# Graph network kernel, layer three: three sign rows on two row groups of TensorE in place of one block of 67 rows

## The reference

```
h = maximum(layernorm(x), 0)
x = x + L2(h, adj)

# inside L2, for every pair of nodes i, j (c = 1):
sub   = mobius_add(-h_i, h_j)
arg   = clip(norm(sub), 0, 1 - 1e-5)
log   = 2 / lam_i * arctanh(arg) * sub / norm(sub)
agg_i = sum_j (adj_ij / deg_i) * log_ij
```

## Time and profile before

| what | value |
|---|---|
| median of three runs | 1149.5 us |
| the profiled execution's own time | 1147.67 us |
| its span, first to last instruction | 1145.9 us |
| TensorE busy, share of the span | 1076.3 us, 94% |
| VectorE busy | 874.6 us, 76% |
| ScalarE busy | 765.6 us, 67% |
| GpSimd busy | 269.2 us, 23% |
| mean granted clock of TensorE | 0.975 of full speed |
| layer three | about 573.5 to 1027 us |

### The profile page before, as it was taken

The page is one execution under the profiler, slowest core; times in us unless marked ns, Lnnn a source line. Parts: engine busy times, 40 slices in busy tenths (PEclk is TensorE's granted clock), DMA queues, the critical chain, the costliest instruction groups (busy, mean ns, idle before and its releaser), DMA issues.

```text
span 1145.9 us, 14188 instructions
## 1 busy us (share of the span) xinstructions
PE 1076.3 (94%) x5084; PEld 486.4 (42%) x5084; DVE 874.6 (76%) x1003; ACT 765.6 (67%) x800; POOL 269.2 (23%) x119
## 2 busy tenths in 40 slices
PE   4899999998579999999989999999999999989898
PEld 1233333337533333333345544555555554435454
DVE  6999989985666666697689877677778777876863
ACT  3455555553366666787688898777777878895683
POOL 2289100000100000000034446333333334341000
PEclk9999999998789999999989999999999999999999
DMA  7999999980038888788744435454445435434472
GB/s 273 406 389 347 355 340 342 354 307 19 1 103 281 284 287 285 239 285 279 245 137 150 139 116 183 151 179 148 150 155 173 147 110 165 129 110 138 138 223 55
DMA packets 96322, 238.27 MB, mean 208 GB/s; under 512 B 16384, under 2 KB 45056, under 8 KB 79872
## 3 DMA queue, kind: packets, MB, share of 16 engines
q1 hardware_dynamic: 87040, 220.62, 57.6%
q10 hardware_dynamic: 9216, 16.78, 3.8%
HBM read 219.55 MB, written 17.83 MB: 207 GB/s over the span
## 4 chain that ended last, share of the span: by engine, by line
PE 78%; DVE 12%; ACT 4%; issue 3%; DMA 1%; SPq 1%; DVEq 0%; ACTq 0%
PE PS L498 51%; PE PS L711 9%; PE PS L644 5%; PE PS L645 5%; PE PS L740 4%; DVE TB L1331 1%; DMA ring<-in_adj_t 1%; PE PS L510 1%; DVE work L1756 1%; DVE work L1767 1%; ACT work L1002 1%; PE PS L532 1%; DVE work L1773 1%; PE PS L522 1%; DVE ring L1779 1%
## 5 line engine op out<-in xcount | busy, mean ns | idle before, releaser
L474 POOL TENSOR_TENSOR ring<-work,ring 128x1024 f32<-128x1024 f32 x58 | 137.3, 2368 | 474.5 <-DVE work L1773 474.5
L1457 DVE TENSOR_TENSOR work<-work,ring 128x1024 f32<-128x1024 f32 x128 | 151.2, 1222 | 75.3 <-ACT work L1002 75.0
L939 ACT ACTIVATE work<-PS 128x1024 uint8<-128x1024 f32 x128 | 124.1, 1021 | 120.3 <-PE PS L498 120.3
L1002 ACT ACTIVATE work<-PS,att_sc 128x1024 f32<-128x1024 f32 x128 | 147.6, 1201 | 78.8 <-PE PS L645 71.4
L498 PE MATMUL PS<-ring,work 128*65 128x256 f32 (+1 forms) x600 | 192.4, 469 | 6.8 <-DVE work L1800 6.8
L498 PE MATMUL PS<-work 128*64 128x512 f32 (+1 forms) x656 | 167.4, 556 | 2.4 <-DVE work L1750 2.4
L1767 DVE SCALAR_TENSOR_TENSOR work<-PS,work 128x1024 f32<-128x1024 f32 x72 | 88.1, 1223 | 88.5 <-PE PS L498 83.2
L711 PE MATMUL PS<-TB,TA 65*128 65x512 f32 x288 | 138.0, 601 | 0.0
L498 PEld LDWEIGHTS PS<-ring,work 128*65 128x65 f32 x600 | 82.0, 139 | 95.5 <-issue 71.6
L644 PE MATMUL PS<-work 128*128 128x512 f16 x256 | 99.0, 387 | 4.8 <-DVE work L1280 3.1
L1066 ACT ACTIVATE work<-work 128x1024 f32<-128x1024 f32 x72 | 75.9, 1054 | 39.9 <-DVE work L1761 39.9
(11 more groups left out here) (237 smaller groups left out, 1493.9 us busy)
## 6 DMA issues: line engine op xcount, KB each, us to landing
ring<-in_adj_t SPq DMA_DIRECT2D x96, 1024.0 KB, 5.2
ring<-in_adj_t SPq DMA_DIRECT2D x104, 512.0 KB, 4.1
work<-in_adj_t SPq DMA_DIRECT2D x32, 1024.0 KB, 7.8
codes<-work ACTq DMA_DIRECT2D x64, 256.0 KB, 6.7
ring<-codes SPq DMA_DIRECT2D x64, 256.0 KB, 3.1
H<-in_adj_t SPq DMA_DIRECT2D x24, 512.0 KB, 4.0
X<-in_x SPq DMA_DIRECT2D x2, 512.0 KB, 5.2
out_x<-X SPq DMA_DIRECT2D x1, 512.0 KB, 4.1
```

The source lines that it names most:

```text
L474: nc.gpsimd.tensor_tensor(near(n), sums(n), near(n), ALU.mult).then_inc(sem("near_ready"), 1)
L939: nc.scalar.activation(made[:, k, u * UNIT:(u + 1) * UNIT], PS[:, (4 + 2 * u) * BANK:(6 + 2 * u) * BANK], ACT.Relu).then_inc(sem("codes_ma ...
L1002: nc.scalar.activation(att[:, u, :], PS[:, (4 + 2 * u) * BANK:(6 + 2 * u) * BANK], ACT.Sigmoid, bias=att_sc[:, 2:3], scale=att_sc[:, 1:2]) ...
L1457: V.tensor_tensor(prob[:, m % 4, :], att[:, u, :], ring[:, s % RING, u * UNIT:(u + 1) * UNIT], ALU.mult)\
```

## The change

The sign matmuls use three rows only. For the pair's even tile they lie on partitions 0 to 2, for the odd tile on partitions 64 to 66, which are different row groups of the array. So `kap_l` is filled every other tile at the top and every other tile below, and `kap_r` is made twice, once for each place. Where one instruction of 67 rows made a piece, there are two of three rows: two copies of half as many elements and two multiplies of as many as before. On GpSimd each of the four waits for the one before, and the first for its own product of that unit. The counts that semaphores wait for are doubled.

```diff
+        TOP, LOW = slice(0, ROWS - D), slice(D, ROWS)
+        def every_other(ap, odd):
+            return ap.rearrange("r (p q n) -> r p q n", q=2, n=P)[:, :, odd, :]
...
             def sign_rows(r):
                 c = slice(HALF + r * UNIT, HALF + (r + 1) * UNIT)
                 pool.wait_ge(sem("zr_out"), 2 + r + 1)
-                nc.gpsimd.tensor_copy(kap_l[0:ROWS, c], TB[0:ROWS, c]).then_inc(sem("kap_ready"), 1)
-                nc.gpsimd.tensor_scalar(kap_r[0:ROWS, c], TB[0:ROWS, c], kmask[0:ROWS, 0:1], None, ALU.mult)\
-                  .then_inc(sem("kap_ready"), 1)
+                pool.wait_ge(sem("near_ready"), FLIPS[r] + 2)
+                for odd, rows in ((0, TOP), (1, LOW)):
+                    k = 4 * r + 2 * odd
+                    nc.gpsimd.tensor_copy(every_other(kap_l[rows, c], odd), every_other(TB[LOW, c], odd))\
+                      .then_inc(sem("kap_ready"), 1)
+                    pool.wait_ge(sem("kap_ready"), k + 1)
+                    nc.gpsimd.tensor_scalar(kap_r[rows, c], TB[LOW, c], kmask[LOW, 0:1], None, ALU.mult)\
+                      .then_inc(sem("kap_ready"), 1)
+                    pool.wait_ge(sem("kap_ready"), k + 2)
...
             def sides2(n):
...
-                for q in range(2):
-                    ins = add(z_banks(n)[:, q * BANK:(q + 1) * BANK], kap_l[0:ROWS, (2 * p + q) * P:(2 * p + q + 1) * P],
-                              kap_r[0:ROWS, S * STRIP:(S + 1) * STRIP])
+                for q, rows in ((0, TOP), (1, LOW)):
+                    ins = add(z_banks(n)[:, q * BANK:(q + 1) * BANK], kap_l[rows, (2 * p + q) * P:(2 * p + q + 1) * P],
+                              kap_r[rows, S * STRIP:(S + 1) * STRIP])
...
-                    nc.scalar.activation(kap_r[0:ROWS, c], TB[0:ROWS, c], ACT.Copy, scale=kmask[0:ROWS, 0:1])\
-                      .then_inc(sem("kap_r_ready"), 1)
+                    for rows in (TOP, LOW):
+                        nc.scalar.activation(kap_r[rows, c], TB[LOW, c], ACT.Copy, scale=kmask[LOW, 0:1])\
+                          .then_inc(sem("kap_r_ready"), 1)
...
-                    V.tensor_copy(kap_l[0:ROWS, r * UNIT:(r + 1) * UNIT], PS[0:ROWS, 0:UNIT]).then_inc(sem("kap_l_ready"), 1)
+                    for odd, rows in ((0, TOP), (1, LOW)):
+                        V.tensor_copy(every_other(kap_l[rows, r * UNIT:(r + 1) * UNIT], odd), every_other(PS[LOW, 0:UNIT], odd))\
+                         .then_inc(sem("kap_l_ready"), 1)
```

More of the change, by code:

```diff
@@ L673, in first_half1 @@
                     pe.wait_ge(sem("zl_out"), 1)
-                    pe.wait_ge(sem("kap_l_ready"), 1)
+                    pe.wait_ge(sem("kap_l_ready"), 2)
                     flip_rows(PS[0:ROWS, 0:UNIT], TG // 2, TG).then_inc(sem("z_flipped"), 1)
@@ L700, in scores2 @@
                     pe.wait_ge(sem("zl_out"), 2)
-                    pe.wait_ge(sem("kap_l_ready"), 2)
+                    pe.wait_ge(sem("kap_l_ready"), 4)
                 if n < ROT:
@@ L718, in sides2 @@
                 if n == 0:
-                    pe.wait_ge(sem("kap_r_ready"), 2)
+                    pe.wait_ge(sem("kap_r_ready"), 4)
                 if n in (N0, N0 + TG // 4):
-                    pe.wait_ge(sem("kap_ready"), 2 + 2 * (n - N0) // (TG // 4))
-                for q in range(2):
-                    ins = add(z_banks(n)[:, q * BANK:(q + 1) * BANK], kap_l[0:ROWS, (2 * p + q) * P:(2 * p + q + 1) * P],
-                              kap_r[0:ROWS, S * STRIP:(S + 1) * STRIP])
+                    pe.wait_ge(sem("kap_ready"), 4 + 4 * (n - N0) // (TG // 4))
+                for q, rows in ((0, TOP), (1, LOW)):
+                    ins = add(z_banks(n)[:, q * BANK:(q + 1) * BANK], kap_l[rows, (2 * p + q) * P:(2 * p + q + 1) * P],
+                              kap_r[rows, S * STRIP:(S + 1) * STRIP])
                 ins.then_inc(sem("side_ready"), 1)
```

## The result

The changed kernel takes 1153.7 us (median of 5 runs, 1152.84 to 1155.55), the kernel before 1149.05 (5 runs on the same chip, 1148.56 to 1149.94). The ratio is 1.0045, 95% interval 1.0032 to 1.0058: slower, by 4.7 us between the medians and by 5.2 us as the ratio has it. Of the profiled executions the spans are 1151.1 and 1145.9 us, 5.2 apart too. All lines of the changed kernel stand some way further down: the matmul helper is L510 (was L498), scores L723, transposes L752, VectorE's three steps L1776 (was L1761), L1782 and L1788, its addition L1815, GpSimd's product L486, its casts L470 and multiplies L473.

What follows compares the result with a forecast made beforehand. Layer three was taken as bound by TensorE's instruction stream nearly everywhere. Stall less overlap +2.0, layer two's rows 0 and GpSimd's rows +3.0 gave +5.0 us, 1154.5; forecast's own range 1151 to 1161, 8-in-10 range 1139 to 1161.

Steps and rivals of the forecast that it cites:

- Part 1: Sign matmul pair on TensorE: the two three-row matmuls run at once on separate row groups, saving 0.22 us a unit.
- Part 2: TensorE around the pair: switching from whole array to split and back stalls, costing 0.26 us a unit.
- (a): Rival for TensorE around the pair: row groups need no stall, so 8.0 us faster, 1141.5; chance 0.27.
- (b): Rival for TensorE around the pair: half a stall, 0.11 us a round trip, 2.5 us faster, 1147; chance 0.10.
- (c): Rival for the pair on TensorE: it stalls and doesn't overlap, +16 us, 1165.5; chance 0.06.
- 50 units at 0.04: Layer three units bound by TensorE: each pays the stall less the overlap, +0.04 us net, +2.0 us in all.
- Part 3: Making the rows in layer two on ScalarE and VectorE: extra work hidden, cost nothing; 1.5 us without cover.
- Part 4: Making the rows on GpSimd in layer three: 3.9 us more work, twice, costing +3.0 us; bounds 0 and +6.
- rival (d): Rival on GpSimd's row making: stall as forecast, GpSimd's extra work hidden, +2.0 us, 1151.5; chance 0.07.
- the ways to fail: Round trip under 0.16 us, GpSimd's three-partition multiply not 3.3 us, or longer waits slowing TensorE behind them.
- up to 1 us may come from here instead: First sign_rows call: VectorE work beside GpSimd's longer multiply slows by up to 1 us; 1.0 taken for the call.
- GpSimd busy 8 to 9 us per sign_rows: Sign of GpSimd's extra work in the profile after: each sign_rows call keeps GpSimd busy 8 to 9 us.

Runs made afterwards that it cites:

- the part alone: Kernel before with its 67-row sign matmuls, but GpSimd making its rows in four instructions with a wait between each: 1151.22 us, ratio 1.0026.
- 3 and 3 alone: Kernel before with the two sign matmuls on three rows each, on row groups 0 and 2, rows made as before: 1151.43 us, ratio 1.0025.
- 32 and 32: Kernel before with the pair of sign matmuls on two tiles of 32 rows, partitions 0 to 31 and 32 to 63: 1150.75 us, ratio 1.0026.
- 64 and 3: Kernel before with the even tile's sign matmul on 64 partitions and the odd tile's on the three sign rows: 1169.22 us, ratio 1.0186.
- the two kernels with GpSimd's copy: Changed kernel with GpSimd's second multiply replaced by a bf16 copy: 1154.84 us; the same with the second sign_rows call behind unit 21: 1153.91 us.

## Why the prediction came out right

It said 1154.5 us and slower, 5.0 us over the kernel before; measured were 1153.7, with 4.7 us between the medians and 5.2 by the ratio. By its own steps:

**Part 1**, the pair side by side: as predicted, 0.39 in place of 0.60, and with three rows on one group it is 0.60 again.

**Part 2**, the round trip: the 0.26 us, taken from a column split in another layer, holds for rows: 0.25 with three rows or 64 on one group, 6.51 for the unit. Scores to pair came out at 0.52 for the last one (1.81 less three times 0.43; 0.53 predicted), pair to transposes 0.32 (0.31), the eight transposes 1.09 as said. Rivals (a) and (b), a stall of none or half, are out by the same rows, and so is (c), by the 0.39 us of the pair. The run with three rows on one group is what (c) would have been, without GpSimd's part: the +13 us of its stalls came out as 12.9, and the clock added 3.3.

The term's size was too high in what reached the end: 50 units at 0.04 were to give 2.0 us. What is left of layer three's 6.0 us after units 20 to 22 (3.3), unit 39 (1.6) and the fall near 970 (0.3) is 0.8. Of the 71 distances from pair to pair, 53 grew by 0.02 to 0.04 us each, 1.8 in all, so the cost in the stream is the forecast's. Eight others grew shorter, by 0.95 together, and six of those hold a wait of TensorE that the kernel before has too. TensorE's waits for VectorE's last product fell from 5.5 us in 7 to 3.9 in 5, as the waits show:

```profile
PE PS L510 <- DVE work L1815: 4.6, 1, 4.6
PE PS L752 <- DVE work L1788: 3.9, 5, 1.2
...
PE PS L510 <- POOL ring L486: 0.7, 1, 0.7
```

So half of the delay was taken out of waits and passages that were there before. The prediction had charged its 50 units in full and given nothing back for the other 22.

**Part 3**, layer two: hidden, 247.5 us on both sides.

**Part 4**, GpSimd: predicted +3.0, measured +3.3 in units 20 to 22 of the changed kernel. With the part alone it was +3.0 by the ratio and 3.7 in layer three of its trace, 0.4 of that ahead of sides2(20), which waited for the rows. So rival (d) is out. The place of the cost was off. The prediction gave 1.0 us to the first call and 2.0 to the second. The first cost 3.1: TensorE's wait grew from 1.87 to 4.64, and the lower clock behind it cost some 0.5 us, which the prediction names among the ways to fail and doesn't price. The second cost 0.2: the wait for near(20), 0.73 in place of the 1.5 forecast, took the place of one of 0.56. That the two errors cancel is luck. The step that was mis-sized is "up to 1 us may come from here instead" for VectorE: its scaling of rows took 2.1 us longer and L1776 another 0.85, in series and in the chain that TensorE waits for. near(18) itself, named as 0.8 us late, was done at 694.72, before VectorE's addition at 696.32 began, so it did not hold up the gather itself; it did so by what it does to VectorE beside it. "GpSimd busy 8 to 9 us per sign_rows" came out at 7.6 for the first call (684.39 to 691.97) and 8.3 for the second.

**Left out of the sum**: the clock. The prediction saw it only behind long waits. It fell in unit 39, with no wait, for 1.6 us, and cost 0.3 near 970. That the total still agreed is partly luck: part 2 reached the end with 1.2 us less than forecast, and the clock took 1.9. In layer three alone the profiled execution is 6.0 us longer, 1.0 more than forecast; that it began the layer 0.8 us earlier is scatter.

## What to carry to other kernels

Count the switches before using row groups: here a round trip from the whole array and back costs 0.25 us, one overlapped matmul of 512 columns gives back 0.22, and a lone pair loses. By these numbers two pairs of one tile size behind each other would win 0.19 us; that is an estimate, and no run here shows a gain. Before lengthening work on GpSimd, look at what VectorE runs beside it and who waits for that, not only at what is queued on GpSimd. And when a matmul is made smaller, read the granted clock of the steady stretches afterwards: one fall cost 1.6 us, and the pair's 0.035 us a unit came to 0.8 in all.

## What the runs showed of the hardware that was not expected

TensorE's granted clock fell to its half level in a stretch where the engine was busy 10.00 of 10.00 us, at the same unit in both traces of the changed kernel. It fell in that unit 39 also with three rows on one row group, with 3 and 3 alone, with 32 and 32 and with 64 and 3. It did not with 67 or 64 rows in both matmuls, nor in the two kernels with GpSimd's copy, whose pair has three rows. Eight transposes then take 1.97 us in place of 1.09.

VectorE's f32 multiplies by a scalar ended a fixed time behind the GpSimd instruction that they ran beside. GpSimd's end, then VectorE's: 691.97 and 692.52, 694.72 and 695.27 in the changed kernel; 694.58 and 695.13 in the one with the copy. That is 0.55 us each time, where alone the two take 0.69 and 0.74. Beside GpSimd's products of two tensors it is so in all of layer three of the kernel before, of the changed one and of that with the copy, 0.54 to 0.59 us (in the kernel before 704.48 and 705.03). Beside GpSimd's multiplies it is not always so, as in this row of the changed kernel, while GpSimd's multiply ran from 704.39 to 707.23:

```profile
705.59 0.69 DVE L1776 TENSOR_SCALAR work<-work 128x1024 f32<-128x1024 f32 x1
```

What tells the two cases apart stays open. The Trainium skill (Advanced Engine Details and Errata, VectorE Performance Modes, Mode Summary) says that VectorE's second port is shared with GpSimd, and that two-port modes and GpSimd's instructions block each other. The trace agrees where the multiply is put off: the whole instruction comes later, and is not slowed in proportion. The row above is a case in which it was not blocked.
